# Beta added early in a wavelet stage, its affine work reordered, and expert weights issued in the routing stage

## The reference

```python
def _L1_attn_ref(x, h_filter, g_filter, h_synth, g_synth, norm_gamma, norm_beta):
    low, highs, lens = x, [], []
    for _ in range(2):
        lens.append(low.shape[1])
        highs.append(dwconv(low, g_filter)[:, ::2])
        low = dwconv(low, h_filter)[:, ::2]
    low = linear_attention(low, 16)
    for h, L in zip(reversed(highs), reversed(lens)):
        up_l = jnp.repeat(low, 2, axis=1)[:, :L]
        up_h = jnp.repeat(h, 2, axis=1)[:, :L]
        low = dwconv(up_l, h_synth) + dwconv(up_h, g_synth)
    return layer_norm(x + low, norm_gamma, norm_beta)

x = _layernorm(x + _L1_attn_ref(x, ...), axis=-1)
x = _layernorm(x + _L1_ffn_ref(x, ...), axis=-1)    # top-2 of 8 experts, with a capacity
```

## Time and profile before

| what | value |
|---|---|
| median of 3 runs | 2051.96 us (2049.16 to 2056.83) |
| the profiled execution | 2052.82 us |
| its span in the profile | 2050.7 us |
| PE busy | 1783.5 us, 87% of the span |
| DVE busy | 1151.2 us, 56% |
| ACT busy | 893.4 us, 44% |
| POOL busy | 420.6 us, 21% |

### The profile page before, as it was taken

One profiled execution on the slowest core, in us unless ns is written; L12 is line 12 of the kernel. 1 busy time (PEld: TensorE's weight loads), 2 busy tenths in 40 slices (PEclk: granted clock), 3 DMA queues, 4 the chain that ended last, 5 costly groups with the idle time before them and its releaser, 6 DMA issues. The chain is left out here.

```text
span 2050.7 us, 36532 instructions
## 1 busy us (share of the span) xinstructions
PE 1783.5 (87%) x11248; PEld 1140.2 (56%) x11249; DVE 1151.2 (56%) x2478; ACT 893.4 (44%) x1315; POOL 420.6 (21%) x567
## 2 busy tenths in 40 slices
PE   7889999999999999987479999999999399726762
PEld 4523444444444444446368888888888348726541
DVE  4578888888888888836811111111111586966224
ACT  3426666666666666664022323323233251120323
POOL 2210000000000000012023333333333100001782
PEclk9969999999999999999789999999999699865996
DMA  4511111111111111116533344443433200061445
GB/s 152 173 60 32 34 37 31 31 31 35 35 31 31 35 35 31 31 56 199 185 113 114 94 120 106 105 115 93 121 102 82 87 1 1 1 236 49 51 46 165
DMA packets 103316, 158.32 MB, mean 77 GB/s; under 512 B 20832, under 2 KB 79520, under 8 KB 97888
## 3 DMA queue, kind: packets, MB, share of 16 engines
q1 hardware_dynamic: 74128, 123.71, 18.5%
q0 software_dynamic: 22656, 24.51, 7.6%
q10 hardware_dynamic: 6480, 9.44, 1.4%
HBM read 123.15 MB, written 49.02 MB: 84 GB/s over the span
## 5 line engine op out<-in xcount | busy, mean ns | idle before, releaser
L548 DVE TENSOR_REDUCE unit_max<-ps_ring 128x1 f32<-128x512 f32 x1024 | 639.3, 683 | 70.9 <-PE ps_ring L423 64.9
L534 ACT ACTIVATE w<-ps_scores 128x1024 f32<-128x1024 f32 x512 | 503.8, 1023 | 265.5 <-PE ps_scores L500 262.7
L423 PE MATMUL ps_ring<-k_stack,q_stack 96*128 96x512 bf16 x1024 | 367.4, 393 | 21.2 <-POOL v_padded L386 9.5
L500 PE MATMUL ps_scores<-q_stack,k_stack 98*128 98x512 bf16 x1024 | 307.3, 382 | 2.6 <-ACT w L534 2.5
L1447 PE MATMUL m_ps_h<-m_xt,m_w 128*128 128x256 f32 x1248 | 277.3, 381 | 0.8 <-DVE m_xt L1498 0.8
L1459 PE MATMUL m_ps_y<-w,m_ht 128*128 x1248 | 275.8, 379 | 0.0
L445 PE MATMUL ps_o<-w,v_padded 128*32 128x256 f32 x4096 | 261.1, 384 | 0.0
L1447 PEld LDWEIGHTS m_ps_h<-m_xt,m_w 128*128 128x128 f32 x1248 | 238.1, 191 | 33.8 <-DVE m_xt L1498 1.2
L1459 PEld LDWEIGHTS m_ps_y<-w,m_ht 128*128 128x128 f32 x1248 | 234.2, 190 | 30.3
L423 PEld LDWEIGHTS ps_ring<-k_stack,q_stack 96*128 96x128 bf16 x1024 | 98.7, 97 | 262.0 <-DVE unit_max L548 177.0
L1479 ACT ACTIVATE m_ht<-m_ps_h,m_w 128x256 f32<-128x256 f32 x312 | 131.0, 471 | 143.3 <-PE m_ps_h L1447 143.3
(11 more groups left out here) (256 smaller groups left out, 1670.3 us busy)
## 6 DMA issues: line engine op xcount, KB each, us to landing
m_w<-in_w SPq DMA_DIRECT2D x39, 1028.0 KB
rows<-g_rows SPq DMA_DIRECT2D x16, 512.0 KB, 3.0
y<-sums SPq DMA_DIRECT2D x16, 512.0 KB, 6.8
q_parts<-qk_part SPq DMA_DIRECT2D x16, 384.0 KB, 3.6
k_parts<-qk_part SPq DMA_DIRECT2D x16, 384.0 KB, 3.9
q_stack<-q_parts SPq DMA_DIRECT2D x64, 96.0 KB
k_stack<-k_parts SPq DMA_DIRECT2D x64, 96.0 KB
xt<-in_xt ACTq DMA_DIRECT2D x8, 512.0 KB, 4.3
```

The costliest lines, as they stand in the source:

```text
L423: nc.tensor.matmul(out[:, :], qs[0:STACK, u, qt * P:(qt + 1) * P], ks[0:STACK, u, half * HALF:(half + 1) * HALF], start=True, stop=True).t ...
L500: mm = nc.tensor.matmul(p_s[kt % 2][:, half * HALF:(half + 1) * HALF], ks[:, u, kt * P:(kt + 1) * P], qs[:, u, half * HALF:(half + 1) * HALF],
L534: nc.scalar.activation(pt[:, kt, :], p_s[kt % 2][:, :], ACT.Exp, scale=SCALE)\
L548: nc.vector.tensor_reduce(unit_max[:, u % 2, half, qt:qt + 1], src[:, :], axis=AX.X, op=ALU.max).then_inc(ring_used, 1)
```

## The change

1. The sum of x and beta is written to a space of its own, `shifted` (the space of `c.xe` for sequences 0 and 1 and of `c.xo` for 2 and 3), in place of x2. `shift(0)` is issued after attention 1, behind a wait for `high_made` 8, and shifts 1 to 3 after tiles 0, 1 and 2.
2. `scales` is split in `variances` (seven operations) and `scales` (six). The new order is attention 0, 1, shift 0; tiles 0 to 3 with shifts 1 to 3 between them, variances 0, scales 0, attention 2; tiles 4 to 7, variances 1, affine (0, first half), scales 1, attention 3, affine (0, second half); tiles 8 to 11, variances 2, affine (1, first), scales 2, affine (1, second); tiles 12 to 15, variances 3, affine (2, first), scales 3, affine (2, second); both halves of affine 3.
3. The weights are no longer issued by SP in `stage_gate`, but by ACT in `stage_route`, after the exponential.

```diff
-                if late_loads:
-                    late_loads(sp)
...
+        shifted = [x[:, :, :, :].rearrange("p c b n -> p (c b n)")[:, 0:NT // 2 * D].rearrange("p (i d) -> p i d", d=D)
+                   for x in (c.xe, c.xo)]
...
+                def shift(b):
+
+                    v.tensor_tensor(shifted[b // 2][:, b % 2 * TB:(b % 2 + 1) * TB, :], c.x2[:, b * TB:(b + 1) * TB, :],
+                                    bcast(beta[:, :].unsqueeze(1), [P, TB, D]), ALU.add)
...
-                    x2 = c.x2[:, cut, :]
-                    v.tensor_tensor(x2, x2, bcast(beta[:, :].unsqueeze(1), [P, TB, D]), ALU.add)
...
-                        link(v.tensor_tensor(y, y, x2, ALU.add))
+                    link(v.tensor_tensor(y, y, shifted[b // 2][:, of_half:of_half + HB, :], ALU.add))
...
-                for s in range(B + 1 + 1):
-                    if s < B:
-                        attention(s)
-                    if s > 1:
-                        affine(s - 1 - 1)
-                    if 1 <= s < B + 1:
-                        tiles(s - 1)
-                        scales(s - 1)
+                dve.wait_ge(high_made, B * KC)
+                shift(0)
+                for b in range(B):
+                    for i in range(b * PAIRS, (b + 1) * PAIRS):
+                        tile(i)
+                        if i < B - 1:
+                            shift(i + 1)
+                    variances(b)
+                    if b > 0:
+                        affine(b - 1, 0)
+                    scales(b)
+                    if b + 2 < B:
+                        attention(b + 2)
+                    if b > 0:
+                        affine(b - 1, 1)
+                for h in range(2):
+                    affine(B - 1, h)
...
-            stage_gate(nc, c, a.gate_1, rows[1], weight_loads)
-            stage_route(nc, c, CAP * E, CAP, rows[1], sums[1])
+            stage_gate(nc, c, a.gate_1, rows[1])
+            stage_route(nc, c, CAP * E, CAP, rows[1], sums[1], weight_loads)
```

More of the change, by code:

```diff
@@ L815, in normalised, with stage_gate @@
                                    c.rstd[:, bass.ds(i, 1)], c.nmr[:, bass.ds(i, 1)], ALU.mult, ALU.add)
-def stage_gate(nc, c, wgate, rows, late_loads=None):
+def stage_gate(nc, c, wgate, rows):
     HB, HALVES, BUFS, TURNS = TB // 2, 2 * B, 4, 6
@@ L1764, in attention, with tile, variances @@
                     last.then_inc(syn2_ready, 1)
[L1766 to L1779, removed]
+                def tile(i):
+                    dve.wait_ge(tile_made, i + 1)
+                    v.tensor_tensor(c.y[:, 2 * i:2 * i + 2, :].rearrange("p a d -> p (a d)"), banks[i % 4][:, :],
+                                    c.x2[:, 2 * i:2 * i + 2, :].rearrange("p a d -> p (a d)"), ALU.add)\
+                        .then_inc(tile_used, 1)
+                    dve.wait_ge(tile_used, i + 1)
+                    for j in range(2):
+                        last = row_stats(nc, c, 2 * i + j)
+                    if i % PAIRS == PAIRS - 1:
+                        link(last)
+                def shift(b):
+                    v.tensor_tensor(shifted[b // 2][:, b % 2 * TB:(b % 2 + 1) * TB, :], c.x2[:, b * TB:(b + 1) * TB, :],
+                                    bcast(beta[:, :].unsqueeze(1), [P, TB, D]), ALU.add)
+                def variances(b):
                     cut = slice(b * TB, (b + 1) * TB)
                     even, odd = c.six[:, cut, 1], c.six[:, cut, 4]
-                    mean, rstd, nmr = c.mean[:, cut], c.rstd[:, cut], c.nmr[:, cut]
+                    mean = c.mean[:, cut]
                     v.tensor_tensor(var[:, :], c.six[:, cut, 2], c.six[:, cut, 5], ALU.add)
@@ L1791, in scales @@
                     v.tensor_tensor(var[:, :], var[:, :], tmp[:, :], ALU.add).then_inc(var_ready, 1)
-                    x2 = c.x2[:, cut, :]
-                    v.tensor_tensor(x2, x2, bcast(beta[:, :].unsqueeze(1), [P, TB, D]), ALU.add)
+                def scales(b):
+                    cut = slice(b * TB, (b + 1) * TB)
+                    mean, rstd, nmr = c.mean[:, cut], c.rstd[:, cut], c.nmr[:, cut]
                     dve.wait_ge(root_ready, b + 1)
@@ L1802, in scales, with affine @@
                         .then_inc(scale_ready, 1)
[L1804 to L1809, removed]
-                        link(v.tensor_tensor(y, y, x2, ALU.add))
-                        for i in range(at, at + HB):
-                            row_stats(nc, c, i)
-                dve.wait_ge(affine_loaded, 32)
-                for s in range(B + 1 + 1):
-                    if s < B:
-                        attention(s)
-                    if s > 1:
-                        affine(s - 1 - 1)
-                    if 1 <= s < B + 1:
-                        tiles(s - 1)
-                        scales(s - 1)
+                def affine(b, h):
+                    at, of_half = b * TB + h * HB, (b % 2 * 2 + h) * HB
+                    y = c.y[:, at:at + HB, :]
+                    dve.wait_ge(norm_ready, 2 * b + h + 1)
+                    link(v.tensor_tensor(y, y, bcast(gamma[:, :].unsqueeze(1), [P, HB, D]), ALU.mult))
+                    link(v.tensor_tensor(y, y, shifted[b // 2][:, of_half:of_half + HB, :], ALU.add))
+                    for i in range(at, at + HB):
+                        row_stats(nc, c, i)
+                attention(0)
+                attention(1)
+                dve.wait_ge(affine_loaded, 32)
+                dve.wait_ge(high_made, B * KC)
[15 more added lines that the diff above has]
+                    affine(B - 1, h)
             @block.scalar
@@ L2182, in build, with weight_loads @@
             loaded = m.sem("loaded_1")
[L2184 to L2188, removed]
+            def weight_loads(act):
+                act.dma_start(w1[:, :, :], a.w1_1.rearrange("e (c p) f -> p (e c) f", p=P)).then_inc(loaded, 16)
+                act.dma_start(w2[:, :, :], a.w2_1.rearrange("e (c p) f -> p (e c) f", p=P)).then_inc(loaded, 16)
+                act.dma_start(b1[:, :], a.b1_1).then_inc(loaded, 16)
+                act.dma_start(b2[:, :, :], a.b2_1.partition_broadcast(P)).then_inc(loaded, 16)
             stage_rstd(nc, c)
-            stage_gate(nc, c, a.gate_1, rows[1], weight_loads)
-            stage_route(nc, c, CAP * E, CAP, rows[1], sums[1])
+            stage_gate(nc, c, a.gate_1, rows[1])
+            stage_route(nc, c, CAP * E, CAP, rows[1], sums[1], weight_loads)
             with nc.Block() as block:
```

## The result

The changed kernel takes 2041.61 us in the median of 5 runs (2039.91 to 2044.59). The ratio to the kernel before, run again beside it, is 0.9946, with a 95% interval of 0.9932 to 0.9961: some 11 us less (8 to 14), where 13.0 less was forecast. One of the five runs of the kernel before took 2244.82 us, where the others took 2049.16 to 2056.83; it was a slow one and is not in the ratio. The profiled execution took 2043.92 us, with a span of 2041.8 in place of 2050.7.

A forecast was written before the change was run, and what follows sets the result against it. Bounds were read per stage: VectorE's backlog in the wavelet's second half, SyncE's weight issue at the gate's end. Savings of 7.6 + 5.45 = 13.0 us from 2051.96 gave 2039.0 us; own range 2035 to 2043, with rivals 2033 to 2047.

The forecast's parts named there:

- The sums with beta in the early gaps, at no cost: Wavelet: four sums of 2.28 us each fit VectorE's waits before tiles 0 to 3, costing nothing; uncovered, 8.8 us.
- VectorE's list added up from tile 7 on: Wavelet: from tile 7 at 1744.00, VectorE's operation prices add up to an end at 1798.54 in place of 1806.13.
- What carries the 7.6 us: Wavelet saving of 7.6 us; half an affine after the last scales was to remove VectorE's two 2.14 us waits for ScalarE.
- The end of the gate: Gate to routing: without SyncE's weight issue, VectorE's gap of 5.81 us falls to 0.36, 5.45 us less.
- The loads hidden in ScalarE's list: Routing: weights issued behind ScalarE's exponential cost nothing, landing some 28 us after the stage began, needed some 50 us after.
- The sum: Whole kernel: wavelet 7.6 plus gate 5.45 makes 13.0 us less, so 2039.0 us; chance 0.63.
- The spread: Forecast's own range, 2035 to 2043 us: expert stage's slow stretches shift by 1 to 3 us, runs spread over 7.7.
- the rival that priced it: Expert stage falls to the lower clock: 4.4 us per slow first product, 2061 us at five more slow experts; chance 0.04.
- TensorE falls behind: Wavelet rival: TensorE waits before tile 12 and its clock falls; the wavelet gives 7.6 - 4, time 2043 us; chance 0.16.
- the wavelet gives nothing: Wavelet rival: shifts slow down or a supposed backlog is a fixed wait; only 5.45 us stay, 2046.5 us; chance 0.06.
- the weights are late: Expert stage rival: weights land after 1892 where the estimate is 1857, making the kernel slower; chance 0.03.
- The clock rises in routing: Routing rival: the map's 128 matmuls leave the lower clock, up to 5.3 us more gained, 2033.7 us; chance 0.08.

The follow-up runs named there:

- e5: Changed kernel with the early sums with beta kept but VectorE's other work in the old order; ratio to the kernel before 0.9951, wavelet stretch 88.1 us (changed kernel 87.9).
- e6: Changed kernel with the new order kept but the sums with beta made late, in place in x2; ratio to the kernel before 0.9976, wavelet stretch 94.1 us.
- e1: Kernel before with only the weight loads moved to ACT in the routing stage, wavelet order as before; ratio to the kernel before 0.9972.
- e10: Changed kernel with 18 idle matmuls ahead of the map's products in layer 1's routing; single run, first routing operation to first gather 51.11 us (changed kernel 51.69).
- e12: Changed kernel with VectorE's wavelet gaps filled and idle matmuls before and in layer 1's routing map; median 2033.72 us, ratio to the kernel before 0.9907.
- e11: Changed kernel with 18 idle matmuls before layer 1's routing map and one ahead of every fourth product; ratio to the kernel before 0.9916, routing 46.39 us.

## Why the prediction was right

The forecast was 13.0 us less, and the measured 11 (8 to 14) holds it.

*The sums with beta in the early gaps, at no cost*: right. Four operations of 2.27 to 2.28 us, with TensorE's tiles where they were. In the other space they cost what they cost in place.

*VectorE's list added up from tile 7 on*: right to 0.04 us (1798.54 worked out, 1798.50 measured), each mark on the way too: tile 7 at 1744.00 and 1743.94, tile 15 at 1779.68 and 1779.68, the gap before it 0.3 and 0.27.

*What carries the 7.6 us*: here my account said more than it knew. Of half an affine standing behind the last scales, so that ScalarE has time before affine 3, I wrote "this is what removes the two waits of 2.14", as a condition that holds the 7.6. The new order removes them, but e5 keeps both and loses only 0.2 us, and e6 shows the order alone at 1.4. My own sum held this: VectorE "meets tiles 4 to 7 as they come" means 4.8 us of new waiting, which I did not set against the 4.3 saved.

*The end of the gate*: right. A gap of 0.36, in the changed kernel and in e1, as in the earlier trace rows.

*The loads hidden in ScalarE's list*: right. 20.8 us of issue, nobody behind them, R unchanged in every kernel that has them (but for e10 to e12, where the map itself was changed). They had landed in good time too: the DMA share is 0.96 from 1844 to 1850 and 0.01 from 1850 to 1860, so some 29 us behind the start of routing, for 28 estimated.

*The sum*: 13.0 us forecast, 12.8 up to the first gather. The missing 0.2 lie within what the stretch from the last statistics to the last gate copy varies by itself, 22.4 to 23.7 us (22.68 here, 22.39 before).

*The spread*: the forecast allowed the expert stage 1 to 3 us either way. It was 3.0 between the two profiled executions, and the change's trace had the bad end. But the rival that priced it, 4.4 us for each expert with a slow first product, was mis-sized: it took TensorE for the limit of that stage. The limit is GpSimd's list of gathers and scatters, and slow matmuls count only ahead of the first and the last expert's scatters.

*TensorE falls behind*, *the wavelet gives nothing* and *the weights are late* did not happen. *The clock rises in routing* did not happen by itself in any of the traces without idle matmuls (421 ns each time); e11 shows that its price, 5.3 us, was right. The Trainium skill ("TensorE: Matmul & The Clock Gate", Part 1: The HAM clock gate) has it that sustained matmul activity releases the throttle. The traces agree for the idle matmuls ahead of the map in e10 (granted clock 0.50 when they began, 1.00 by 1840), and not for the map's products, which ran back to back for 27.6 us of the changed kernel at 0.50.

## What to carry to other kernels

Early in this stage the engine that was late at its end had idle gaps, and work without inputs from the stage belongs there; that was 7.4 of the wavelet's 7.6 us. When an order written by hand removes a wait, look for the wait that comes in its place: adding up one engine's list against the other's pace gave every one here to a few hundredths. Before pricing a slower or faster engine in a stage, find the list that has no gap in it (here GpSimd's), for only what delays that list counts.

## What the runs showed of the hardware that was not expected

TensorE busy for 27.6 us on end, with products of 80 columns between weight loads of 128, stayed at 1.2 GHz in every trace without idle matmuls in the routing. When the clock had been brought to 2.4 GHz first, it fell after two pauses of 1.81 and 0.82 us, and 24 us of such products did not bring it back (e10). With one idle matmul of 256 columns for every four products it stayed up (e11 and e12), at no cost to the stage. Issued from ScalarE, the same four loads took 20.8 us to issue, and 10.1 from SyncE; in the first case SyncE issued the copy of rows to sums from 1821.46 to 1824.44, beside the first of them, in the second only just after them (from 1834.25), so the traces don't say whether it is the engine or the company.
